# State stage of a Mamba layer: the copies of last columns two units later, the spread of C behind one more y addition, and four PSUM banks for the preparation of the first chunk

## The chip, the cores and the metric

The kernel runs on one core of a Trainium2 chip, as one program of five instruction streams: TensorE (PE), ScalarE (ACT), VectorE (DVE), GpSimd (POOL) and the DMA queues (SP). The metric is the device time of one execution in microseconds (us).

## The reference, cut to what matters

Six layers follow each other on x of shape (1, 1024, 256). The change touches the fifth, a Mamba layer:

```python
x = x + 0.5 * ffn(norm(x)); x = x + attention(norm(x)); x = x + 0.5 * ffn(norm(x))
x = x + 0.5 * moe(norm(x)); x = x + mamba(norm(x));     x = x + 0.5 * moe(norm(x))

# mamba, with DI = 512 inner channels, DN = 16 states, DR = 128
xz = h @ in_proj.T;  x, z = xz[..., :512], xz[..., 512:]
x_conv = silu(causal depthwise conv of x, 4 taps)
x_dbl = x_conv @ x_proj.T;  dt_low, Bm, Cm = split(x_dbl, [128, 16, 16])
delta = softplus(dt_low @ dt_proj.T + dt_bias);  A = -exp(A_log)
for l in range(1024):                       # the scan, for each channel d and state n
    hst[d, n] = exp(delta[l, d] * A[d, n]) * hst[d, n] + delta[l, d] * Bm[l, n] * x_conv[l, d]
    y[l, d] = sum_n hst[d, n] * Cm[l, n]
out = ((y + x_conv * D) * silu(z)) @ out_proj.T
```

All of it is in float32; matmuls that need the precision take a high and a low part of each operand and add three products.

## The kernel before

**Tiling.** The 1024 positions are two chunks of 512. Channels lie on the 128 partitions, in four tiles m = 0 to 3. PSUM has eight banks of 128x512 float32.

**Order of the work.** `steps()` yields one list of named steps for the whole program, and each engine runs through the same list and takes the steps that have a part for it, in that order. Waits on semaphores tie the engines together. So the order of this list sets the order on each engine, and an instruction that waits holds up everything behind it on its engine.

**Preparation.** `enter_steps` is the input projection, the convolution (w = 0 to 3, four VectorE instructions each, L1742 and L1744) and its silu (L1298). `dt_side(ch)` is a list of small steps: the high and low parts of x_conv (`xc2`); the product for dt (`xdt`) with its high copy on ScalarE (`dts`, L1302) and low part on VectorE (L1758); the same for B and C (`xbc`, `bct`, L1306 and L1764); the transposes of B and C (`trb`, read by `btx`, L1316); the four dt tiles (`dt`, three matmuls each) with two ScalarE readings each (`dta`, L1311 and L1312); the softplus in two sweeps of ScalarE (`dte`, `dtl`, L1325 and L1330), each with a load of another activation table; delta and delta times x_conv (`du`, L1773 and L1775, VectorE); and the transposes of the latter (`tru`, L424) with their copies (`dut`, L1320). All of these use one PSUM bank, number 7: `wait7` makes each use wait until the one before it in the plan has been read. For chunk 0 `alone` runs the steps of this list one after the other, each with its reader behind it, woven by `mamba_steps` between the input steps of chunk 1. For chunk 1 they run as side work between the units of chunk 0.

**State stage.** `state_steps(ch, side)` runs 64 units: pairs of states (n even, n odd), and within a pair the tiles m = 0 to 3 and in each the even and the odd state. Unit number k has u = k % 8. A unit consists of

- `ea`: exp(delta * A) on ScalarE (L1368); for an odd state it goes into PSUM bank 4 or 5, for an even one into SBUF
- b, which is delta * x_conv * B: for an even state four TensorE matmuls with a diagonal of B (`pb`, L1134, bank 4 or 5), for an odd one a GpSimd product (`bm`, L1916) with the row of B spread over the partitions
- `scan`: the recurrence on VectorE, L1797 for even and L1795 for odd states
- `cm`, one step later (GIVE = 1): the product with the spread row of C, for even states on GpSimd (L1925), for odd ones on VectorE (L1806), which reads C from PSUM bank 6
- `keep`, in the same step, chunk 0 alone: a ScalarE copy of the scan's last column (L1374), which chunk 1 starts from
- `ya`, three steps later (SUM = 3): TensorE adds the product to y in bank m (L1145); a float32 matmul shows as two records

The rows of B and C are spread by TensorE matmuls with a one-hot column: `spB` and `spC` through bank 7 and a ScalarE copy (L1115, L1337, L1344), and `bringC` for the odd states straight into bank 6 (L1122). The latter has to wait for the last product of the odd state before it (n - 2, m = 3), which still reads the bank. The scan of unit k waits for the product and the copy of unit k - 5, whose buffer it reuses, and an `ea` of an odd state or a `pb` waits for the scan two units back, whose bank it takes.

Of the kernel before, what the change touches and what calls it, by code (L numbers as in the profile page):

```python
# [6 lines left out]
F = mybir.dt.float32  # L7
# [279 lines left out]
def alone(side):  # L287
    for now, out in side:
        yield now + (out or [])
# [3 lines left out]
GIVE, SUM = 1, 3  # L293


def state_steps(ch, side):
# [6 lines left out]
    for k in range(n_units + SUM):  # L303
# [52 lines left out]
def build(nc, d):  # L356
# [11 lines left out]
    with ctx:  # L368
# [387 lines left out]
        def tensor_program():  # L756
# [28 lines left out]
            for x, *a in plan:  # L785
# [292 lines left out]
                elif x == "xdt":  # L1078
# [4 lines left out]
                    wait7(x, ch)  # L1083
                    pe.wait_ge(*xcd.at(ch, 3))
                    group(bank(7), [q for k in range(4) for q in three([w[:, k, 0:P] for w in X3], [v[:, k, :] for v in XC2])]).then_inc(*xdd.inc(ch))
                elif x == "xbc":
                    ch, = a
                    wait7(x, ch)
                    group(bank(7)[0:64, :], [q for k in range(4) for q in three([w[:, k, P:P + 64] for w in X3], [v[:, k, :] for v in XC2])]).then_inc(*xbd2.inc(ch))
                elif x == "dt":  # L1090
                    ch, m = a
                    wait7(x, ch, m)
                    if m == 0:
                        pe.wait_ge(*dtl.at(ch))
                    group(bank(7), three([w[:, m, :] for w in D3], DT)).then_inc(*dtm.inc(ch, m))
                elif x == "trb":
                    ch, = a
                    wait7(x, ch)
                    pe.wait_ge(*bcl.at(ch))
                    for i in range(TC):  # L1100
                        t = turn_over(bank(7)[:, i * P:i * P + P], BCs[ch][:, i * P:i * P + P].bitcast(F))
                    t.then_inc(*trb.inc(ch))
                elif x == "tru":
                    ch, i = a
                    wait7(x, ch, i)
                    if i == 0:
                        pe.wait_ge(*dud.at(ch, 3))
                    for m in range(4):
                        t = turn_over(bank(7)[:, m * P:m * P + P], uu[ch][:, m, i * P:i * P + P])
# [6 lines left out]
                elif x == "bringC":  # L1116
                    ch, n = a
                    if n > 1:
# [47 lines left out]
        ring7 = [x for x in plan if x[0] in after7]  # L1166

        def wait7(*here):
            k = ring7.index(here)
            if k:  # L1170
                name, *key = ring7[k - 1]
                out, done = after7[name]
                assert plan.index((out, *key)) < plan.index(here)
                pe.wait_ge(*done.at(*key))


        def scalar_program():
            for x, *a in plan:
# [120 lines left out]
                elif x == "dts":  # L1299
                    ch, = a  # L1300
                    act.wait_ge(*xdd.at(ch))
                    act.activation(DT[0], bank(7), ACT.Copy).then_inc(*dth.inc(ch))  # L1302
                elif x == "bct":
                    ch, = a
                    act.wait_ge(*xbd2.at(ch))
                    act.activation(BCs[ch][0:64, :], bank(7)[0:64, :], ACT.Copy).then_inc(*bch.inc(ch))  # L1306
                elif x == "dta":
# [3 lines left out]
                    act.activation(dl[ch][:, m, :], bank(7), ACT.Abs, bias=b)  # L1311
                    act.activation(uu[ch][:, m, :], bank(7), ACT.Relu, bias=b).then_inc(*dab.inc(ch, m))  # L1312
                elif x == "btx":
                    ch, = a
                    act.wait_ge(*trb.at(ch))
                    act.activation(BTh, bank(7).rearrange("p (t n) -> p t n", t=TC)[:, :, 0:64], ACT.Copy).then_inc(*btc.inc(ch))  # L1316
                elif x == "dut":
                    ch, i = a
                    act.wait_ge(*tru.at(ch, i))
                    act.activation(DUT[ch][i], bank(7), ACT.Copy).then_inc(*dut.inc(ch, i))  # L1320
# [60 lines left out]
        def vector_program():  # L1381
# [6 lines left out]
            for x, *a in plan:  # L1388
# [366 lines left out]
                elif x == "dts":  # L1755
                    ch, = a
                    dve.wait_ge(*dth.at(ch))
                    dve.tensor_tensor(DT[1], bank(7), DT[0].bitcast(F), ALU.subtract).then_inc(*dtl.inc(ch))  # L1758
                elif x == "bct":
# [4 lines left out]
                    dve.tensor_tensor(bc[32:64, :], bank(7)[32:64, :], bc[32:64, :].bitcast(F), ALU.subtract).then_inc(*bcl.inc(ch))  # L1764
# [247 lines left out]
```

## Time and profile before

| | us |
|---|---|
| median of 3 runs (lowest, highest) | 1063.16 (1059.86, 1063.55) |
| the profiled execution, its own time | 1064.1 |
| its span | 1062.8 |
| TensorE busy in the span (matmuls) | 763.3 (72%) |
| VectorE busy | 638.6 (60%) |
| ScalarE busy | 392.9 (37%) |
| GpSimd busy | 315.6 (30%) |
| mean granted TensorE clock | 0.843 of full speed |

All durations in the prediction come from the one profiled execution; its time includes 1.3 us around the span. The busy shares are means over stages with different limits, so they say little about one stage. The Mamba layer lies between about 560 and 928 us of the span. TensorE runs at one of two clock levels, 1.2 and 2.4 GHz; the granted clock is the mean share of the full speed in a stretch. In the rows a name such as FB<-PS is the tile written and the tile read, PS is PSUM, and "idle before" is in square brackets with the instruction that ended it. "Issue" means that the profile shows nothing that the engine waited for.

### The profile page before, as it was taken

Reading aid. Unit: us, or ns where it says so; the run is one execution under the profiler, and the core shown is the slowest. Engines: PE = TensorE matmul, PEld = TensorE weight load, DVE = VectorE, ACT = ScalarE, POOL = GpSimd, SP = SyncE. Lnnn points to the kernel's source line nnn. Section 1 sums busy time; section 2 is a strip of 40 time slices with the busy share of each in tenths; the row PEclk is TensorE's granted clock in tenths of the full one; section 3 lists DMA queues with packets and bytes.
Section 4 is the critical chain, followed back from the end, with each engine's and each line's share of the span. In section 5 each row is a group of like instructions: output and inputs, shape, how many; then the busy total and the mean of one; then the engine's idle time right before and its main releaser. Section 6 shows DMA issues by size and latency. Waiting matters only on the chain. (4 is left out here: it accounts for less than half of the span.)

```text
span 1062.8 us, 11266 instructions
## 1 busy us (share of the span) xinstructions
PE 763.3 (72%) x3818; PEld 547.8 (52%) x3818; DVE 638.6 (60%) x1069; ACT 392.9 (37%) x784; POOL 315.6 (30%) x373
## 2 busy tenths in 40 slices
PE   2866877589889597869329368678857888776980
PEld 2655654555554386758227135345535444465870
DVE  4976456665663385634256455588876878763332
ACT  3313353205556232223114544756443454120330
POOL 1241124100112210500320024357634567214005
PEclk9987599857999798889759568879979999968995
DMA  4600000000000230146310000000050000013334
GB/s 166 193 1 0 1 1 1 1 1 1 1 1 1 101 137 31 60 159 198 104 31 0 0 1 1 1 1 1 1 236 3 0 1 1 0 41 126 122 130 118
DMA packets 27816, 52.36 MB, mean 49 GB/s; under 512 B 2288, under 2 KB 22128, under 8 KB 26608
## 3 DMA queue, kind: packets, MB, share of 16 engines
q1 hardware_dynamic: 24688, 43.25, 11.6%
q0 software_dynamic: 3072, 8.39, 2.6%
q8 instruction: 32, 0.52, 0.2%
q14 instruction: 24, 0.20, 0.1%
HBM read 34.20 MB, written 17.43 MB: 49 GB/s over the span
## 5 line engine op out<-in xcount | busy, mean ns | idle before, releaser
L1145 PE MATMUL PS<-FB,C 128*128 128x512 f32 x256 | 135.4, 639 | 1.2 <-DVE FB L1806 1.2
L1241 ACT ACTIVATE FA<-PS 128x512 f32<-128x512 f32 (+3 forms) x192 | 82.7, 497 | 63.0 <-PE PS L922 61.9
L1888 POOL TENSOR_SCALAR_AFFINE_SELECT FA<-FA 128x128 f32<-128x128 f32 x128 | 36.9, 298 | 192.3 <-ACT FA L1241 190.7
L1925 POOL TENSOR_TENSOR FB<-FB,RBF 128x512 f32<-128x512 f32 x51 | 65.8, 1289 | 87.6 <-DVE FB L1797 87.6
L424 PE MATMUL PS<-C,FB 128*128 128x128 f32 x250 | 45.7, 307 | 56.2 <-DVE FB L1438 38.1
L897 PE MATMUL PS<-RA 128*128 128x128 f32 (+3 forms) x288 | 79.9, 402 | 4.1 <-DVE FA L1529 1.3
L922 PE MATMUL PS<-RA 128*128 128x512 f32 (+3 forms) x192 | 66.6, 408 | 17.0 <-ACT FA L1241 8.0
L897 PEld LDWEIGHTS PS<-RA 128*128 128x128 f32 x288 | 56.1, 242 | 31.3 <-DVE FA L1533 13.4
L424 PEld LDWEIGHTS PS<-C,FB 128*128 128x128 f32 x250 | 36.3, 160 | 68.1 <-DVE FB L1438 39.3
L1906 POOL DMA_INDIRECT FB<-GY,FB x32 | 30.6, 955 | 135.6 <-DMA GY<-FB 126.6
L1916 POOL TENSOR_TENSOR FB<-WE,FB 128x512 f32<-128x512 f32 x32 | 43.0, 1344 | 69.0 <-ACT FB L1337 69.0
L1045 PE MATMUL PS<-WE,FB 128*128 x248 | 62.7, 398 | 0.0
L1145 PEld LDWEIGHTS PS<-FB,C 128*128 128x128 f32 x256 | 46.7, 201 | 29.1 <-issue 16.3
L1684 DVE TENSOR_TENSOR FB<-FB,PS 128x256 f32<-128x256 f32 (+1 forms) x32 | 13.2, 412 | 72.7 <-ACT FB L1273 72.7
L922 PEld LDWEIGHTS PS<-RA 128*128 128x128 f32 x192 | 35.1, 201 | 39.6 <-ACT FA L1241 23.5
L420 PE MATMUL PS<-XN,RB 128*128 128x512 f32 x192 | 52.4, 435 | 2.1 <-DVE RB L1386 2.1
L1134 PEld LDWEIGHTS PS<-RBF,WE 128*128 128x128 f32 x256 | 36.8, 212 | 30.9 <-issue 14.0
L1045 PEld LDWEIGHTS PS<-WE,FB 128*128 128x128 f32 x248 | 46.9, 200 | 6.5 <-issue 0.8
L1134 PE MATMUL PS<-RBF,WE 128*128 128x128 f32 x256 | 38.7, 300 | 14.7 <-DVE FB L1797 11.1
L1533 DVE TENSOR_REDUCE FA<-PS 128x1 f32<-128x640 f32 (+2 forms) x48 | 44.3, 953 | 8.1 <-PE PS L897 7.8
L424 PE MATMUL PS<-C,RA 128*128 128x128 f32 x192 | 32.2, 326 | 21.9 <-ACT RA L1220 11.4
L1189 ACT ACTIVATE XN<-PS 128x512 fp32r<-128x512 f32 x24 | 13.6, 594 | 89.5 <-PE PS L424 89.4
(269 smaller groups left out, 1772.0 us busy)
## 6 DMA issues: line engine op xcount, KB each, us to landing
FB<-GX SPq DMA_DIRECT2D x14, 512.0 KB, 4.8
GY<-FB SPq DMA_DIRECT2D x14, 512.0 KB, 3.2
WE<-in_wr SPq DMA_DIRECT2D x4, 1536.0 KB, 11.3
WE<-in_wr SPq DMA_DIRECT2D x3, 2048.0 KB, 13.0
GX<-FA SPq DMA_DIRECT2D x1, 3968.0 KB, 14.0
FA<-in_w SPq DMA_DIRECT2D x2, 1024.0 KB, 7.6
FB<-in_we SPq DMA_DIRECT2D x4, 384.0 KB, 3.5
X<-in_x SPq DMA_DIRECT2D x2, 512.0 KB, 8.5
```

Source lines behind the costliest of these rows:

```text
L420: last = pe.matmul(out, a, b, start=start and i == 0, stop=stop and i == len(pairs) - 1, skip_group_check=skip)
L424: return pe.matmul(out, in_, ident, start=True, stop=True, is_transpose=True)
L897: return pe.matmul(out, QT[:, 4 * (g % 2) + hh, ii * P:ii * P + P], KT[:, 2 * g + hh // 2, c0:c1], start=start, stop=stop)
L922: pe.matmul(bk[:, c0:CH], KT[:, 2 * g + hh // 2, kt * P:kt * P + P], QT[:, 4 * (g % 2) + hh, c0:CH], start=True, stop=True).then_inc(*scs. ...
L1045: m = pe.matmul(bk[:, o:o + D], xt[:, o + k * P:o + k * P + P], WE[:, bass.ds(v + k * 256, 256)], start=k == 0, stop=k == 1)
L1134: t = pe.matmul(bank(4 + k % 2)[:, i * P:i * P + P], DUT[ch][i][:, m * P:m * P + P], dg[:, i * P:i * P + P], start=True, stop=True)
L1145: pe.matmul(bank(m), ident, shc[k % 4], start=n == 0, stop=n == DN - 1).then_inc(*yad.inc(ch, n, m))
L1241: act.activation(PT[n % 16][:, c0:], bank(4 + ring_no[(x, *a)] % 3)[:, c0:], ACT.Exp, scale=0.25).then_inc(*exd.inc(*a))
L1533: r = dve.reduce_max(N3[:, i, h:h + 1], bk.rearrange("p b n -> p (b n)")[:, 0:w], AX)
L1888: pool.affine_select(out=dd, in_=dd, compare_op=ALU.is_ge, fill=0.0, base=0, pattern=[[1, P]], channel_multiplier=-1).then_inc(*sel.inc(*a))
L1916: pool.tensor_tensor(sbb[k % 2], uu[ch][:, m, :], bs[(stb.no[ch, n] - 1) % 2], ALU.mult).then_inc(*bmd.inc(ch, n, m))
L1925: pool.tensor_tensor(shc[k % 4], sh[k % 5], Cs[(stc.no[ch, n] - 1) % 2], ALU.mult).then_inc(*cma.inc(ch, n, m))
```

## The change

1. `keep` moves from the step after its unit to the third step after it (KEEP = 3).
2. `bringC` was emitted at the step that holds the product of the last odd unit of the pair, which is the first step of the next pair (u = 0). Now it is emitted at the second step of the next pair (u = 1), ahead of that step's `ya`.
3. The preparation of chunk 0 gets an order of its own, `dt_alone`, and its eleven uses of bank 7 go round banks 4, 5, 6 and 7: each waits for the reader of the fourth use before it. The first use of bank 7 after them (the spread of B) waits for the readers of the last four, and the first `bringC` for the reader of the last transposes. Chunk 1's preparation still uses bank 7 alone.

```diff
--- before.py
+++ after.py
@@ -284,13 +284,21 @@
     return side
 
 
-def alone(side):
-    for now, out in side:
-        yield now + (out or [])
+def dt_alone():
+
+    for m in range(4):
+        yield [("xc2", 0, m)]
+    for x in (("xdt", 0), ("xbc", 0), ("dts", 0), ("bct", 0), ("dt", 0, 0), ("dt", 0, 1), ("dta", 0, 0), ("trb", 0), ("dt", 0, 2), ("dta", 0, 1),
+              ("btx", 0), ("dt", 0, 3), ("dta", 0, 2), ("dta", 0, 3), ("dte", 0), ("dtl", 0)):
+        yield [x]
+    for m in range(4):
+        yield [("du", 0, m)]
+    yield [("tru", 0, i) for i in range(TC)]
+    yield [("dut", 0, i) for i in range(TC)]
 
 
 UNITS = [(2 * p + j, m) for p in range(DN // 2) for m in range(4) for j in range(2)]
-GIVE, SUM = 1, 3
+GIVE, SUM, KEEP = 1, 3, 3
 
 
 def state_steps(ch, side):
@@ -314,10 +322,10 @@
         if 0 <= k - GIVE < n_units:
             n, m = UNITS[k - GIVE]
             out.append(("cm", ch, n, m))
-            if ch + 1 < NCH:
-                out.append(("keep", ch, n, m))
-            if n % 2 and m == 3 and n + 2 < DN:
-                out.append(("bringC", ch, n + 2))
+        if ch + 1 < NCH and 0 <= k - KEEP < n_units:
+            out.append(("keep", ch, *UNITS[k - KEEP]))
+        if k > 8 and u == 1 and k < n_units:
+            out.append(("bringC", ch, UNITS[k][0]))
         if 0 <= k - SUM < n_units:
             out.append(("ya", ch, *UNITS[k - SUM]))
         if held:
@@ -336,7 +344,7 @@
 
 def mamba_steps():
     yield [("An",)]
-    yield from weave((chain(enter_steps(0), alone(dt_side(0))), 1), (chain(([] for _ in range(8)), enter_steps(1)), 1))
+    yield from weave((chain(enter_steps(0), dt_alone()), 1), (chain(([] for _ in range(8)), enter_steps(1)), 1))
     yield from state_steps(0, dt_side(1))
     yield [("gate", 0)]
     yield from state_steps(1, leave_side())
@@ -1080,33 +1088,33 @@
                     if ch == 0:
                         pe.wait_ge(*mws.at(4))
                         pe.wait_ge(*xno.at(4, 1, 1))
-                    wait7(x, ch)
+                    bk = claim7(x, ch)
                     pe.wait_ge(*xcd.at(ch, 3))
-                    group(bank(7), [q for k in range(4) for q in three([w[:, k, 0:P] for w in X3], [v[:, k, :] for v in XC2])]).then_inc(*xdd.inc(ch))
+                    group(bk, [q for k in range(4) for q in three([w[:, k, 0:P] for w in X3], [v[:, k, :] for v in XC2])]).then_inc(*xdd.inc(ch))
...
                 elif x in ("spB", "spC"):
                     ch, n = a
@@ -1115,6 +1123,8 @@
                     pe.matmul(bank(7), HOT[:, h:h + 1].broadcast_to([P, P]), BCs[ch], start=True, stop=True).then_inc(*(spb if x == "spB" else spc).inc(ch, n))
                 elif x == "bringC":
                     ch, n = a
+                    if ch == 0 and n == 1:
+                        pe.wait_ge(*dut.at(0, TC - 1))
                     if n > 1:
                         pe.wait_ge(*cmb_.at(ch, n - 2, 3))
                     elif ch:
@@ -1163,15 +1173,30 @@
 
         after7 = {"spB": ("stB", stb), "spC": ("stC", stc), "mo": ("mox", mox), "tr1": ("xn", xno), "xdt": ("dts", dtl), "xbc": ("bct", bcl),
                   "dt": ("dta", dab), "trb": ("btx", btc), "tru": ("dut", dut)}
-        ring7 = [x for x in plan if x[0] in after7]
+        early7 = [x for x in plan if x[0] in after7 and x[1] == 0 and x[0] in ("xdt", "xbc", "dt", "trb", "tru")]
+        ring7 = [x for x in plan if x[0] in after7 and x not in early7 and x[0] not in ("xn",)]
+
+        def bank7(*here):
+            return bank(4 + early7.index(here) % 4) if here in early7 else bank(7)
+
+        def emptied(use, here):
+            name, *key = use
+            out, done = after7[name]
+            assert plan.index((out, *key)) < plan.index(here)
+            pe.wait_ge(*done.at(*key))
 
         def wait7(*here):
             k = ring7.index(here)
-            if k:
-                name, *key = ring7[k - 1]
-                out, done = after7[name]
-                assert plan.index((out, *key)) < plan.index(here)
-                pe.wait_ge(*done.at(*key))
+            for use in ring7[k - 1:k] if k else early7[-4:]:
+                emptied(use, here)
+
+        def claim7(*here):
+
+            if here not in early7:
+                wait7(*here)
+            elif early7.index(here) > 3:
+                emptied(early7[early7.index(here) - 4], here)
+            return bank7(*here)
 
 
         def scalar_program():
@@ -1299,25 +1324,25 @@
                 elif x == "dts":
                     ch, = a
                     act.wait_ge(*xdd.at(ch))
-                    act.activation(DT[0], bank(7), ACT.Copy).then_inc(*dth.inc(ch))
+                    act.activation(DT[0], bank7("xdt", ch), ACT.Copy).then_inc(*dth.inc(ch))
...
```

TensorE, turn from one pair of states to the next (L1134 is the b product of an even unit, L1115 the spread of B, L1122 the spread of C, L1145 a y addition), before:

```order
L1134 MATMUL PS<-RBF,WE 128x128 x4
L1115 MATMUL PS<-RB,HOT 128x512
L1122 MATMUL PS<-RB,HOT 128x512
L1145 MATMUL PS<-FB,C 128x512 x2
L1134 MATMUL PS<-RBF,WE 128x128 x4
L1145 MATMUL PS<-FB,C 128x512 x2
L1134 MATMUL PS<-RBF,WE 128x128 x4
```

and now, where the same instructions have the lines L1144, L1123, L1132 and L1155:

```order
L1144 MATMUL PS<-RBF,WE 128x128 x4
L1123 MATMUL PS<-RB,HOT 128x512
L1155 MATMUL PS<-FB,C 128x512
L1132 MATMUL PS<-RB,HOT 128x512
L1155 MATMUL PS<-FB,C 128x512
L1144 MATMUL PS<-RBF,WE 128x128 x4
L1155 MATMUL PS<-FB,C 128x512 x2
L1144 MATMUL PS<-RBF,WE 128x128 x4
```

One y addition has moved from behind the spread of C to ahead of it.

VectorE, preparation of chunk 0 (TENSOR_SCALAR and SCALAR_TENSOR_TENSOR are the convolution of chunk 1, the first TENSOR_TENSOR into RB the low part for dt, the 64x512 and 32x512 ones the low part of B and C, the one into RBF the sum of the transposed B, the one into WE the first of delta), before:

```order
L1742 TENSOR_SCALAR FB<-FB,C 128x512 x4
L1758 TENSOR_TENSOR RB<-PS,RB 128x512
L1744 SCALAR_TENSOR_TENSOR FB<-FB,C 128x512 x4
L1762 MEMSET RB 64x512
L1764 TENSOR_TENSOR RB<-PS,RB 32x512
L1744 SCALAR_TENSOR_TENSOR FB<-FB,C 128x512 x4
L1768 TENSOR_TENSOR RBF<-RBF 128x64
L1744 SCALAR_TENSOR_TENSOR FB<-FB,C 128x512 x4
```

and now:

```order
L1767 TENSOR_SCALAR FB<-FB,C 128x512 x4
L1769 SCALAR_TENSOR_TENSOR FB<-FB,C 128x512 x8
L1783 TENSOR_TENSOR RB<-PS,RB 128x512
L1769 SCALAR_TENSOR_TENSOR FB<-FB,C 128x512 x4
L1787 MEMSET RB 64x512
L1789 TENSOR_TENSOR RB<-PS,RB 32x512
L1793 TENSOR_TENSOR RBF<-RBF 128x64
```

The low part for dt stands behind eight convolution instructions (two of the sweeps) that followed it before, and that of B and C behind the whole convolution. On ScalarE the four silus of chunk 1 now stand ahead of the first reading of a dt tile, where they stood behind it, and the reading of the transposed B behind two dt tiles.

## Rows read from the trace of the kernel before

**Rows 1.** Busy time by stretch: us, PE, PEld, DVE, ACT, POOL, PEclk, DMA share, GB/s
```profile
578.00:624.00 46.00, 21.90 (x70) 13.09 (x68) 17.27 (x30) 23.07 (x39) 1.30 (x1) 0.62 0.00 0
624.00:770.00 146.00, 111.91 (x450) 68.73 (x451) 109.77 (x117) 79.91 (x194) 81.60 (x63) 0.89 0.00 1
785.00:916.00 131.00, 107.35 (x452) 64.50 (x451) 103.36 (x115) 57.67 (x106) 81.20 (x65) 0.93 0.10 41
```

**Rows 2.** Waits, state stage of chunk 0: waiter, releaser, us in total, times, longest
```profile
ACT SM L1374 <- DVE FB L1795: 21.2, 17, 3.9
...
PE PS L1122 <- DVE FB L1806: 16.5, 7, 5.2
```

**Rows 3.** Waits, state stage of chunk 1
```profile
PE PS L1122 <- DVE FB L1806: 14.0, 7, 2.3
```

**Rows 4.** Preparation in time: start, us, engine, line, what, count, [idle before <- releaser]
```profile
578.13 1.67 DVE L1742 TENSOR_SCALAR FB<-FB,C 128x512 f32<-128x512 f32 x4
...
582.05 0.69 DVE L1758 TENSOR_TENSOR RB<-PS,RB 128x512 fp32r<-128x512 f32 x1 [2.25 <-ACT RB L1302]
582.66 2.73 DVE L1744 SCALAR_TENSOR_TENSOR FB<-FB,C 128x512 f32<-128x512 f32 x4
...
591.05 2.29 ACT L1298 ACTIVATE FB<-FB 128x512 f32<-128x512 f32 x4
...
594.55 1.65 PE L420 MATMUL PS<-RB 128*128 128x512 f32 x3 [1.69 <-ACT WE L1312]
...
600.52 1.28 ACT L1325 ACT_TABLE_LOAD   x1
...
611.53 1.09 PE L424 MATMUL PS<-C,WE 128*128 128x128 f32 x4 [12.33 <-DVE WE L1775]
...
616.90 1.11 PE L424 MATMUL PS<-C,WE 128*128 128x128 f32 x4 [0.69 <-ACT WE L1320]
```

**Rows 5.** Transposes back to back elsewhere, TensorE in time
```profile
935.78 1.97 PE L424 MATMUL PS<-C,FB 128*128 128x128 f32 x8 [0.79 <-DVE FB L1438]
```

**Rows 6.** One turn of chunk 0 (k=40 to k=42), all engines in time
```profile
728.58 1.20 DVE L1797 TENSOR_TENSOR_SCAN FB<-RBF,PS 128x512 f32<-128x512 f32 x1
...
729.69 0.66 DVE L1806 TENSOR_TENSOR FB<-RBF,PS 128x512 f32<-128x512 f32 x1
...
729.99 0.71 ACT L1368 ACTIVATE FB<-WE,SM 128x512 f32<-128x512 f32 x1
...
730.41 0.50 PE L1122 MATMUL PS<-RB,HOT 128*128 128x512 f32 x1 [1.94 <-DVE FB L1806]
...
730.75 1.88 PE L1145 MATMUL PS<-FB,C 128*128 128x512 f32 x4
731.11 1.29 POOL L1916 TENSOR_TENSOR FB<-WE,FB 128x512 f32<-128x512 f32 x1
...
732.46 1.05 PE L1134 MATMUL PS<-RBF,WE 128*128 128x128 f32 x8
...
733.61 1.22 DVE L1797 TENSOR_TENSOR_SCAN FB<-FB,PS 128x512 f32<-128x512 f32 x1 [2.12 <-issue]
```

**Rows 7.** The additions behind the spread at five other turns, TensorE in time
```profile
669.78 2.89 PE L1145 MATMUL PS<-FB,C 128*128 128x512 f32 x4
...
799.62 3.02 PE L1145 MATMUL PS<-FB,C 128*128 128x512 f32 x4
...
824.05 3.56 PE L1145 MATMUL PS<-FB,C 128*128 128x512 f32 x4
...
858.15 3.52 PE L1145 MATMUL PS<-FB,C 128*128 128x512 f32 x4
...
901.69 2.69 PE L1145 MATMUL PS<-FB,C 128*128 128x512 f32 x4
```

**Rows 8.** The spread ahead of the fourth of these
```profile
857.82 0.50 PE L1122 MATMUL PS<-XN,HOT 128*128 128x512 f32 x1 [2.07 <-DVE FB L1806]
```

**Rows 9.** A turn of chunk 1 with a shorter wait
```profile
842.84 0.50 PE L1122 MATMUL PS<-XN,HOT 128*128 128x512 f32 x1 [1.27 <-DVE FB L1806]
```

More of the change, by code:

```diff
@@ L1082, in tensor_program @@
                         pe.wait_ge(*xno.at(4, 1, 1))
-                    wait7(x, ch)
+                    bk = claim7(x, ch)
                     pe.wait_ge(*xcd.at(ch, 3))
-                    group(bank(7), [q for k in range(4) for q in three([w[:, k, 0:P] for w in X3], [v[:, k, :] for v in XC2])]).then_inc(*xdd.inc(ch))
+                    group(bk, [q for k in range(4) for q in three([w[:, k, 0:P] for w in X3], [v[:, k, :] for v in XC2])]).then_inc(*xdd.inc(ch))
                 elif x == "xbc":
                     ch, = a
-                    wait7(x, ch)
-                    group(bank(7)[0:64, :], [q for k in range(4) for q in three([w[:, k, P:P + 64] for w in X3], [v[:, k, :] for v in XC2])]).then_inc(*xbd2.inc(ch))
+                    bk = claim7(x, ch)
+                    group(bk[0:64, :], [q for k in range(4) for q in three([w[:, k, P:P + 64] for w in X3], [v[:, k, :] for v in XC2])]).then_inc(*xbd2.inc(ch))
                 elif x == "dt":
                     ch, m = a
-                    wait7(x, ch, m)
+                    bk = claim7(x, ch, m)
                     if m == 0:
                         pe.wait_ge(*dtl.at(ch))
-                    group(bank(7), three([w[:, m, :] for w in D3], DT)).then_inc(*dtm.inc(ch, m))
+                    group(bk, three([w[:, m, :] for w in D3], DT)).then_inc(*dtm.inc(ch, m))
                 elif x == "trb":
                     ch, = a
-                    wait7(x, ch)
+                    bk = claim7(x, ch)
                     pe.wait_ge(*bcl.at(ch))
                     for i in range(TC):
-                        t = turn_over(bank(7)[:, i * P:i * P + P], BCs[ch][:, i * P:i * P + P].bitcast(F))
+                        t = turn_over(bk[:, i * P:i * P + P], BCs[ch][:, i * P:i * P + P].bitcast(F))
                     t.then_inc(*trb.inc(ch))
@@ L1108, in tensor_program @@
                     for m in range(4):
-                        t = turn_over(bank(7)[:, m * P:m * P + P], uu[ch][:, m, i * P:i * P + P])
+                        t = turn_over(bk[:, m * P:m * P + P], uu[ch][:, m, i * P:i * P + P])
                     t.then_inc(*tru.inc(ch, i))
@@ L1305, in scalar_program @@
                     act.wait_ge(*xbd2.at(ch))
-                    act.activation(BCs[ch][0:64, :], bank(7)[0:64, :], ACT.Copy).then_inc(*bch.inc(ch))
+                    act.activation(BCs[ch][0:64, :], bank7("xbc", ch)[0:64, :], ACT.Copy).then_inc(*bch.inc(ch))
                 elif x == "dta":
@@ L1315, in scalar_program @@
                     act.wait_ge(*trb.at(ch))
-                    act.activation(BTh, bank(7).rearrange("p (t n) -> p t n", t=TC)[:, :, 0:64], ACT.Copy).then_inc(*btc.inc(ch))
+                    act.activation(BTh, bank7("trb", ch).rearrange("p (t n) -> p t n", t=TC)[:, :, 0:64], ACT.Copy).then_inc(*btc.inc(ch))
                 elif x == "dut":
@@ L1319, in scalar_program @@
                     act.wait_ge(*tru.at(ch, i))
-                    act.activation(DUT[ch][i], bank(7), ACT.Copy).then_inc(*dut.inc(ch, i))
+                    act.activation(DUT[ch][i], bank7("tru", ch, i), ACT.Copy).then_inc(*dut.inc(ch, i))
                 elif x == "dte":
@@ L1757, in vector_program @@
                     dve.wait_ge(*dth.at(ch))
-                    dve.tensor_tensor(DT[1], bank(7), DT[0].bitcast(F), ALU.subtract).then_inc(*dtl.inc(ch))
+                    dve.tensor_tensor(DT[1], bank7("xdt", ch), DT[0].bitcast(F), ALU.subtract).then_inc(*dtl.inc(ch))
                 elif x == "bct":
@@ L1763, in vector_program @@
                     dve.wait_ge(*bch.at(ch))
-                    dve.tensor_tensor(bc[32:64, :], bank(7)[32:64, :], bc[32:64, :].bitcast(F), ALU.subtract).then_inc(*bcl.inc(ch))
+                    dve.tensor_tensor(bc[32:64, :], bank7("xbc", ch)[32:64, :], bc[32:64, :].bitcast(F), ALU.subtract).then_inc(*bcl.inc(ch))
                 elif x == "btx":
```

6 lines of the change are left out of this document (3 added, 3 removed).

## The prediction

> **What bounds the kernel now.** I read the views in this order: the busy time by stretch, the list of waits of the two state stretches, and then the instructions in order of time in the first chunk's preparation and around one turn from a pair of states to the next. The stretches that the change touches are the preparation of chunk 0 (46 us from 578 to 624), the state stage of chunk 0 (146 us) and that of chunk 1 (131 us) [rows 1]. In the preparation nobody is busy: TensorE 21.9 us, ScalarE 23.1, VectorE 17.3. It is a chain of hand-overs. In both state stretches VectorE (109.8 of 146, 103.4 of 131) and TensorE (111.9 and 107.4) are busiest, TensorE partly because it runs slowly, so what can be won there lies in VectorE's idle spells, 36 and 28 us.
>
> Where do they lie? TensorE waited seven times per chunk in L1122, the spread of C, for the product of VectorE: 16.5 us [rows 2] and 14.0 us [rows 3]. One such place in order of time is [rows 6]. With k the number of the unit, the scan of k=40 starts at 728.58, the product of k=39 runs behind it until 730.35, and only then may L1122 start (730.41, after 1.94 us of idle TensorE). Behind it in TensorE's queue stand two y additions (four records of L1145, 730.75 to 732.46, so 0.86 us for each addition) and the b product of k=42 (L1134, 1.05 us, done at 733.51). The scan of k=42 starts at 733.61, and VectorE had stood idle for 2.12 us before it. The other scans of this piece follow each other without a gap. So the wait that ends last there is TensorE's row of spread, two additions and b product, and its start is fixed by VectorE itself.
>
> **The change part by part.** *The spread of C.* The words of the change say that it goes behind the next pair's first b. The instruction order shows that it stood behind that b before as well; what it passes is one y addition (k=37 in the example) and nothing else. It happens at 14 turns, 7 in each chunk. The addition's input was ready long before, so it now fills part of the 1.94 us of waiting, and only one addition stands between the spread and the b product. Nothing is added, and no wait is new: the wait for the product of k=39 stays in front of the spread, and behind it are one addition, the side work of that unit and the b product. Who needs the spread is the VectorE product of k=41, which comes after the scan of k=42, so it isn't late. Worth: 0.86 us where TensorE runs at full clock, for VectorE's gap shrinks from 2.12 to 1.26 us. At five turns the four records took 2.89, 3.02, 3.56, 3.52 and 2.69 us instead of 1.88 [rows 7], because TensorE's clock fell to its lower level after the wait (the whole stretches were granted 0.89 and 0.93 [rows 1]); there half of the four is saved. A sixth turn, behind the longest wait of 5.2 us [rows 2], ran slowly too, but transposes behind it wait for VectorE's own work, so it counts at the full-clock price. Sum: 9 x 0.86 + (2.89 + 3.02 + 3.56 + 3.52 + 2.69)/2 = 7.7 + 7.8 = 15.5 us. The bound below is 14 x 0.86 = 12.0.
>
> What comes late next at such a turn? The exponential of k=42 is ready at 730.70 and GpSimd's product for k=43 at 732.40, over 2 us before the scan of k=43 would need it even then [rows 6]. Per eight units TensorE has to do 4 b products, 8 additions and 3 spreads, some 4 x 0.86 + 8 x 0.86 + 3 x 0.34 = 11.3 us (0.34 from the start of the spread at 730.41 to that of the addition, 730.75; a b product of 1.05 starts its successor a little before it ends). VectorE's period is eight scans of about 1.21 and four products of 0.66, each starting some 0.09 before the one ahead ends, with the gap of 2.12: 13.4 us now and 12.5 then. So TensorE still keeps up, at full clock.
>
> *The clock.* The idle spell of TensorE in front of the spread falls from about 2.0 us to about 1.1. The drop to the lower clock was seen after 2.07 us [rows 8], while the additions behind the waits of 1.27 us [rows 9] and 1.94 us [rows 6] aren't among the slow ones. If every drop went away, the remaining half of the five slow groups, 7.84 - 5 x 0.94 = 3.1 us, would go, and about as much again for the b products and side matmuls behind them: 6 us. If none goes, 0. I take the middle, 3 us, since 1.94 and 2.07 lie on either side and the new spell is nearer to 1.27. The Trainium skill, "TensorE: Matmul & The Clock Gate", Part 1, says that "the default state is throttled, and activity releases the throttle"; by it the denser queue would keep the full level and the whole 6 us would come. This case's rows don't decide it: spells that are nearly alike were followed by either level.
>
> *The copies of last columns (L1374), two units later.* ScalarE waited 21.2 us in 17 of them for scans [rows 2], but it has 66 us to spare in that stretch [rows 1]. What stands behind such a copy is the exponential for an odd unit, which waits for the same scan anyway (its PSUM bank), or side work whose input comes from TensorE. A copy is needed by the scan five units later, and its new place is still ahead of the exponential that this scan needs. I take 0; bounds from the 0.2 us of a copy and the few waits of VectorE for ScalarE: a gain of 1.5 us to a loss of 0.5.
>
> *Four banks for the preparation of chunk 0.* Two things move. First, the order on VectorE: before, the low part of dt's input (L1758, 582.05) ran between the convolutions of chunk 1, and VectorE idled 2.25 us ahead of it [rows 4]. Now eight convolution steps come first. VectorE is free at 578.13 + 1.67 = 579.8; eight steps at 2.73 for four, less the overlap, are 5.4, to 585.2; then 0.69 to 585.9 (3.2 us later than before); then four more steps to 588.6. The silu of chunk 1 (four in 2.29) follows the steps one by one and is done at about 589.3. Meanwhile TensorE has done the B and C rows without waiting, and from 585.9 the dt groups, 0.7 to 1.65 us each; two are done by 589.3 and none has to wait for a bank that isn't free. From there ScalarE is the bound: eight readings at 0.6 us (the four silus give its pace, 0.57) and the transposed B, 0.4, together 5.2, to 594.5. Before, the next step, the table load for the exponential, started at 600.52 [rows 4]. Gain 6.0.
>
> Second, the four groups of transposes from 611.53 on [rows 4]: one bank makes each wait for the copy before it, so they end at 616.90 + 1.11 = 618.01, 6.5 us after the first began. With four banks they run back to back, at half of 1.97 us each [rows 5], 3.9 us, and the copies follow behind. Gain 2.5. What follows (diagonals, spreads of B and C, the first scan) hangs on the last copy in the same way as before. Preparation together: 8.5 us. Bounds: 5.5, where half-clock dt groups hold up the last reading or a convolution waits, and 9.5.
>
> After the state stages everything is one chain up to the end (gate, projection, expert layer), so the gain isn't given back; the load of the expert weights starts with the gate of chunk 0 and moves with it.
>
> **Sum.** 8.5 + 15.5 + 3 + 0 = 27 us. The profiled execution took 1064.1 us with a span of 1062.8, with 1.3 around it, so it comes to 1037.1; it lay 0.9 above the median of the runs, 1063.16, so I predict 1036.
>
> **Rivals.**
> (a) The clock doesn't recover, or drops in other places, and the turns yield only their full-clock price: 8.5 + 12 = 20.5 us, 1042.7. For it: 1.94 and 2.07 us of idle gave both levels, so the length of that one spell isn't the whole cause.
> (b) The clock stays at its upper level throughout: 8.5 + 15.5 + 6 = 30 us, 1033. Against it: in the preparation TensorE idles for 12.3 us whatever the order [rows 4], and the state stage begins after it.
> (c) Another wait takes the place of the removed one at the turns (GpSimd's product or the exponential): then only the preparation counts, 1063.2 - 8.5 = 1054.7. Against it: the exponential was ready at 730.70 where the b product ended at 733.51 [rows 6].
> (d) Slower: TensorE stays at the lower level for whole pairs of states. Eight units then need about twice 11 us, 22, against 13.4 now: 8.6 us lost in each such period. With 16 periods in the two chunks, more than three further ones wholly at the lower level (27/8.6) would turn the gain into a loss; with five it is 1063.2 - 27 + 43 = 1079. Against it: the change makes TensorE's idle spells shorter, so nothing pushes it there.
>
> **How the numbers follow.** Forecast 0.55, (a) 0.25, (b) 0.12, (c) 0.05, (d) 0.03. With the bounds of the preparation and of the clock, from 5.5 + 12 = 17.5 to 9.5 + 15.5 + 6 + 1.5 = 32.5 us, the times are 1045.7 and 1030.7, and an us more for the executions' own spread gives the range 1030 to 1046. Case (c) and (d) stay outside. Within 0.5% is 1058 to 1068.5, about what a measurement of this kernel can tell from no change; only a mix of (c) and (d) ends there. Faster 0.95, same 0.03, slower 0.02.
>
> **What would show it.** In the changed profile, the seven scans per chunk that follow a turn should stand behind a gap near 1.26 us instead of 2.12, and one addition each should lie on either side of the spread. Table load at about 594.5, and the first scan 8.5 us earlier, if the preparation is right; VectorE's other scans spaced as before. The waits for the spread should add up to some 8 us per chunk instead of 16.5 and 14.0. The granted clock of the two state stretches shows which of forecast, (a) and (b) it is: near 0.95, 0.90 or 1.0. I am wrong if the turns keep their 2.12 us with another engine named behind them, or if the table load comes no earlier than 598.

## The result, and the profile after

| | before | after |
|---|---|---|
| median (lowest to highest), us | 1061.5 (1057.9 to 1063.6), 4 runs | 1032.0 (1027.2 to 1038.8), 4 runs |
| ratio, 95% interval | | 0.971 (0.966 to 0.977) |
| the profiled execution, its span | 1064.1, 1062.8 | 1032.8, 1031.6 |
| mean granted TensorE clock | 0.843 | 0.855 |

The median fell by 29.5 us; 1036 was forecast, in a range of 1030 to 1046. The ratio, here and below, is not the quotient of the two medians, so the two can differ by half a percent.

**Where it came from.** I cut the Mamba layer of both traces at the same four events: first convolution instruction of chunk 1, table load of the softplus, first scan, first gate product (and again the first scan and the gate for chunk 1). The lengths of the stages in us:

| | convolution to table load | to first scan | state stage 0 | between | state stage 1 |
|---|---|---|---|---|---|
| before | 22.4 | 23.3 | 146.0 | 15.2 | 130.7 |
| after | 16.0 | 20.1 | 136.6 | 15.2 | 119.3 |
| gain | 6.4 | 3.2 | 9.4 | 0.0 | 11.5 |

Together 30.5 of the 31.3 us that lie between the two profiled executions. VectorE and the clock in the stretches that answer to [rows 1] (columns as there), each cut at the events of the table:

```profile
578.00:614.63 36.63, 17.17 (x71) 12.09 (x69) 17.54 (x29) 22.81 (x39) 1.30 (x1) 0.74 0.00 0
614.63:751.24 136.61, 107.89 (x450) 65.28 (x450) 109.68 (x116) 77.99 (x194) 81.57 (x63) 0.93 0.00 1
766.41:885.66 119.25, 102.36 (x451) 62.14 (x450) 103.31 (x115) 57.66 (x106) 81.18 (x65) 0.96 0.11 45
```

VectorE idles 27 of 137 us and 16 of 119 where it had idled 36 of 146 and 28 of 131, with the same work done. The granted clock rose from 0.89 to 0.93 and from 0.93 to 0.96.

The waits for the spread of C, answering to [rows 2] and [rows 3], first chunk 0 and then chunk 1 (waiter, releaser, us in total, times, longest):

```profile
PE PS L1132 <- DVE FB L1831: 9.7, 7, 3.5
```
```profile
PE PS L1132 <- DVE FB L1831: 8.5, 7, 1.4
```

16.5 became 9.7 and 14.0 became 8.5, where "some 8 us" each was forecast. One turn of chunk 0 in order of time, answering to [rows 6] (TensorE, VectorE and the exponentials of ScalarE; L1132 is the spread, L1155 an addition, L1144 the b product, L1820 and L1822 the scans, L1831 VectorE's product):

```profile
712.25 1.02 PE L1155 MATMUL PS<-FB,C 128*128 128x512 f32 x2
712.54 1.19 DVE L1822 TENSOR_TENSOR_SCAN FB<-RBF,PS 128x512 f32<-128x512 f32 x1
...
713.65 0.66 DVE L1831 TENSOR_TENSOR FB<-RBF,PS 128x512 f32<-128x512 f32 x1
...
714.23 1.21 DVE L1820 TENSOR_TENSOR_SCAN FB<-PS,FB 128x512 f32<-128x512 f32 x1
...
714.37 0.50 PE L1132 MATMUL PS<-RB,HOT 128*128 128x512 f32 x1 [1.09 <-DVE FB L1831]
...
714.70 1.02 PE L1155 MATMUL PS<-FB,C 128*128 128x512 f32 x2
...
715.48 0.69 ACT L1393 ACTIVATE PS<-WE,SM 128x512 f32<-128x512 f32 x1 [0.82 <-DVE FB L1820]
715.56 1.05 PE L1144 MATMUL PS<-RBF,WE 128*128 128x128 f32 x8
...
716.70 1.22 DVE L1822 TENSOR_TENSOR_SCAN FB<-FB,PS 128x512 f32<-128x512 f32 x1 [1.26 <-ACT PS L1393]
```

One addition stands on either side of the spread, TensorE idles 1.09 us instead of 1.94, and VectorE's gap is 1.26 us instead of 2.12. The releaser that is named for it, the exponential, was done at 716.17; the b product ended at 716.61, and the scan started 0.09 later. The work that ends last there is still TensorE's row.

The preparation, answering to [rows 4]:

```profile
578.48 1.67 DVE L1767 TENSOR_SCALAR FB<-FB,C 128x512 f32<-128x512 f32 x4
...
580.19 5.52 DVE L1769 SCALAR_TENSOR_TENSOR FB<-FB,C 128x512 f32<-128x512 f32 x8
...
585.62 0.68 DVE L1783 TENSOR_TENSOR RB<-PS,RB 128x512 fp32r<-128x512 f32 x1
...
587.00 2.62 ACT L1323 ACTIVATE FB<-FB 128x512 f32<-128x512 f32 x4 [1.86 <-DVE FB L1769]
...
594.52 1.28 ACT L1350 ACT_TABLE_LOAD   x1
...
605.52 3.58 PE L432 MATMUL PS<-C,WE 128*128 128x128 f32 x16 [12.64 <-DVE WE L1800]
```

The idle of 2.25 us ahead of the low part is gone, the table load stands at 594.52, and the sixteen transposes run in one piece of 3.58 us where they had spread over 6.5.

One thing hadn't been forecast: the clock around the first scan. Windows of 6 us ahead of it, of the 8 us behind it, and of the next 8, first before and then after:

```profile
617.84:623.84 6.00, 4.32 (x13) 2.94 (x12) 0.00 (x1) 4.88 (x10) 1.30 (x1) 0.50 0.00 0
623.84:631.84 8.00, 5.19 (x19) 3.40 (x20) 7.93 (x9) 4.08 (x11) 4.47 (x4) 0.64 0.00 0
631.84:639.84 8.00, 4.45 (x15) 2.80 (x14) 7.42 (x9) 3.42 (x9) 3.86 (x3) 0.78 0.00 0
```
```profile
608.63:614.63 6.00, 3.54 (x15) 2.34 (x13) 0.00 (x0) 5.19 (x11) 1.30 (x1) 0.78 0.01 3
614.63:622.63 8.00, 4.97 (x19) 3.40 (x20) 7.93 (x9) 4.36 (x11) 4.47 (x4) 0.72 0.00 0
622.63:630.63 8.00, 4.44 (x19) 2.70 (x18) 7.93 (x10) 2.81 (x7) 3.88 (x3) 1.00 0.00 0
```

Behind the dense transposes TensorE is granted 0.78 ahead of the first scan, not 0.50, and 1.00 instead of 0.78 from 8 us behind it. The ninth scan starts 19.9 us after the first instead of 22.8: 2.9 us that belong to the preparation's change although they are won in the state stage. The ten profiles of this document agree on it. In the five with the four banks TensorE's clock rises to the full level 4.8 to 5.7 us ahead of the first scan, and the ninth scan follows the first by 19.9 us in each; in the five without them it rises 1.5 to 5.7 us behind the first scan, and the ninth scan follows by 22.4 to 22.8 us. It doesn't stay up at once: after the change it is low again from 2.3 us ahead of the first scan to 4.5 behind it, and before the change it was low again from 12.5 to 19.4 us behind it.

### The profile page after: what moved, and what is told of

It is laid out like the page before. It is cut to its first block and busy times, and to the rows that moved or that the text cites. A ratio compares the mean times of both kernels' runs of the same rounds, so it can differ in the third digit from the quotient of the medians.

```text
span 1031.6 us, 11267 instructions
## 1 busy us (share of the span) xinstructions
PE 750.4 (73%) x3818; PEld 542.1 (53%) x3818; DVE 638.6 (62%) x1069; ACT 390.6 (38%) x784; POOL 315.8 (31%) x373
## 5 line engine op out<-in xcount | busy, mean ns | idle before, releaser
L1155 PE MATMUL PS<-FB,C 128*128 128x512 f32 x256 | 132.3, 616 | 1.2 <-DVE FB L1831 1.2
L1155 PEld LDWEIGHTS PS<-FB,C 128*128 128x128 f32 x256 | 45.2, 196 | 20.9 <-issue 10.8
L1144 PEld LDWEIGHTS PS<-RBF,WE 128*128 128x128 f32 x256 | 35.6, 206 | 31.1 <-issue 14.0
L1144 PE MATMUL PS<-RBF,WE 128*128 128x128 f32 x256 | 37.8, 295 | 15.3 <-DVE FB L1822 11.8
```

Source lines behind the costliest of these rows:

```text
L1144: t = pe.matmul(bank(4 + k % 2)[:, i * P:i * P + P], DUT[ch][i][:, m * P:m * P + P], dg[:, i * P:i * P + P], start=True, stop=True)
L1155: pe.matmul(bank(m), ident, shc[k % 4], start=n == 0, stop=n == DN - 1).then_inc(*yad.inc(ch, n, m))
```

## The experiments

The parts were first run singly. The "stages" given with each are cut at the events of the table above, in the same order. Each experiment was timed against the kernel before on the same chip. That kernel's median was 1064.0 us over 19 runs (1053.8 to 1070.9) beside the first four experiments, and 1064.3 over 17 (1058.0 to 1070.4) beside the others.

**The spread of C alone (e1)**, on the kernel before:

```diff
-            if n % 2 and m == 3 and n + 2 < DN:
-                out.append(("bringC", ch, n + 2))
+        if k > 8 and u == 1 and k < n_units:
+            out.append(("bringC", ch, UNITS[k][0]))
```

> The kernel before with the spread of C behind one more y addition, and nothing else. If the spread is worth what the changed kernel's turns show (one addition out of VectorE's gap at each of 14 turns, and TensorE's clock kept up behind the shorter wait): the two state stretches shorter by about 9 and 11 us, the time about 21 us shorter, gaps of 1.26 and 1.20 us at the turns. If the clock recovered only because of the new copies or the new preparation: 12 to 16 us, with some groups of additions still at half rate.

Measured: 1043.3 us (1039.0 to 1046.7), ratio 0.982 (0.975 to 0.990). Stages: 22.4, 23.3, 139.0, 15.2, 118.8. So the preparation is as before, chunk 0 gains 7.0 and chunk 1 gains 11.9: 18.9 us (the ratio's 1.76% of 1064 is 18.7). Gaps at the last four turns of each chunk are 1.26 and 1.20 us. The additions behind the spread are slow at none of the 13 turns other than the third of chunk 0, so the clock's recovery there needs neither the copies nor the preparation. The 21 us of the expectation weren't reached. One reason is the first turn of chunk 0: its gap shrank by 0.87 us, but the stretch from the last scan ahead of it to the same place one pair on took 21.18 us instead of 20.98. The clock fell within it, behind another wait, that of TensorE for the low part of B and C (four transposes; first before, then e1):

```profile
657.72 0.63 PE L424 MATMUL PS<-C,XN 128*128 128x128 f32 x4 [2.52 <-DVE XN L1764]
```
```profile
657.46 1.09 PE L424 MATMUL PS<-C,XN 128*128 128x128 f32 x4 [2.53 <-DVE XN L1764]
```

The work behind the same wait ran at half rate in e1, and VectorE's gap ahead of the scan of k=12 grew from 1.86 to 2.92 us.

**The preparation alone (e2)**: the changed kernel with the old places of the copies and of the spread.

```diff
-        if ch + 1 < NCH and 0 <= k - KEEP < n_units:
-            out.append(("keep", ch, *UNITS[k - KEEP]))
-        if k > 8 and u == 1 and k < n_units:
-            out.append(("bringC", ch, UNITS[k][0]))
+            if ch + 1 < NCH:
+                out.append(("keep", ch, n, m))
+            if n % 2 and m == 3 and n + 2 < DN:
+                out.append(("bringC", ch, n + 2))
```

> The kernel before with the new preparation of chunk 0 alone. If the parts add: table load at about 594.5 and first scan at about 614.6, the state stretches as before, 9 to 10 us shorter in all. If the preparation also shifts TensorE's clock in the state stage, the turns at which additions run at half rate change too, by up to 6 us either way.

Measured: 1043.2 us (1040.8 to 1051.5), ratio 0.986 (0.977 to 0.994). Stages: 16.0, 20.1, 143.8, 15.2, 126.5. The preparation gains its full 9.5 us by itself, and the ninth scan again stands 19.9 us behind the first. Chunk 1, whose order is that of before, came out 4.2 us shorter in this profile. Its waits for the spread are as long as before (2.07 and 2.19 us at the first two turns), yet none of its additions ran slowly. I count that with the clock and not with the order of the work, which is unchanged there: e5, whose preparation has the same four banks, took 132.1 us for chunk 1. That the preparation has no hand in it is not shown, since the other profiles with the old order of chunk 1 (before, e3, e5, e8) took 130.6 to 132.1 us.

**The copies alone (e3)**: KEEP = 3 on the kernel before.

> The kernel before with the copies of last columns two units later, and nothing else. By the theory that nothing that VectorE waits for stands behind such a copy: no change, within 0.5 us in the state stretch of chunk 0. By the rival that ScalarE's waits on scans delay the side work of chunk 1: up to 3 us shorter, with VectorE's gaps behind ScalarE smaller.

Measured: 1062.6 us (1058.1 to 1067.2, 10 runs), ratio 0.999 (0.995 to 1.003). Stages: 22.4, 23.3, 145.7, 15.2, 130.8. ScalarE hardly waits in the copy any more, but waits for the same scans in the exponential that stands behind it, as the list of its waits in chunk 0 shows (L1368 is the exponential; compare the first row of [rows 2]):

```profile
ACT PS L1368 <- DVE FB L1795: 31.5, 18, 5.7
```

All its waits for scans in that stage are 39 us instead of 51, and its waits for products of TensorE 28 us instead of 14: it waits elsewhere, and no less.

**The changed kernel with the copies at their old place (e7)**: KEEP = 1.

> The changed kernel with the copies of last columns back at their old place. If the copies are worth nothing: the same as the changed kernel, the state stretch of chunk 0 within 0.5 us of 136.6. If they matter only once the turns are short: 1 to 3 us longer.

Measured: 1032.1 us (1031.6 to 1036.3), ratio to before 0.970 (0.965 to 0.975), that of the changed kernel being 0.971; state stages 136.6 and 119.2. The stages of the changed kernel are 136.6 and 119.3, so the copies are worth nothing in either company.

**Banks with the old order (e5)**: the changed preparation with `alone(dt_side(0))` in place of `dt_alone()`, spread and copies as before.

```diff
-    yield from weave((chain(enter_steps(0), dt_alone()), 1), ...
+    yield from weave((chain(enter_steps(0), alone(dt_side(0))), 1), ...
```

> The kernel before with the eleven uses of chunk 0's preparation going round four banks, but in the old order (each reader right behind its use, the low part for dt between the convolutions), and nothing else. If the banks free the transposes and lift TensorE's clock, and the order frees the dt tiles: the last four copies end about 2.5 to 3 us earlier relative to the table load, the dt tiles gain some 3 us of the 6 (TensorE runs ahead, ScalarE's readings follow each other), the first scan comes 5.5 to 7 us earlier, and the first nine scans take 2 to 3 us less. If the order alone does it: 2.5 us from the transposes and nothing before the table load.

Measured: 1060.6 us (1050.8 to 1062.9, 10 runs), ratio 0.993 (0.989 to 0.997). Stages: 18.3, 20.2, 146.0, 15.2, 132.1. So of the 6.4 us ahead of the table load 4.1 come from the banks and 2.3 from the new order on top of them (the new order with one bank was not run), and the 3.2 us behind it are the banks'. The ratio's 0.7% is 7.1 us, the preparation's 7.2. The state stages gain nothing in this profile although the first units are 2.9 us quicker here too: three more turns than before ran at the low clock (counted in the next section).

**Filling the wait (e4)**: the kernel before, where the spread of B, which stands ahead of the wait, is issued five times over into the same bank from the second pair on. The wait in front of the spread of C gets shorter, but nothing starts earlier.

```diff
+                    for _ in range(4 if x == "spB" and n > 1 else 0):
+                        pe.matmul(bank(7), HOT[...], BCs[ch], start=True, stop=True)
                     pe.matmul(bank(7), HOT[...], BCs[ch], start=True, stop=True).then_inc(...)
```

> The kernel before, with the matmul that spreads B issued five times over instead of once from the second pair of states on (the same result written to the same bank), which fills about 0.9 us of the wait ahead of the spread of C and moves nothing else. If it is the idle spell that lets the clock fall: the additions behind the spread run at full rate at all turns (1.88 us for four records), VectorE's gaps there are 2.1 us throughout, and the time is 5 to 9 us shorter though TensorE does more. If the clock falls for another cause: the same five slow turns, or others, and 0 to 2 us longer.

Measured: 1058.1 us (1049.3 to 1062.9, 10 runs), ratio 0.995 (0.991 to 0.999), so some 5 us shorter with 56 matmuls more. The state stages took 144.6 and 126.0 us, 1.4 and 4.7 less. The last turn of each chunk has no spread of B left to fill it, and at the third of chunk 0, filled too, the wait is still 3.49 us and the additions are slow. Here are, in chunk 0, a filled turn and the unfilled one (TensorE; the line numbers are shifted, L1124 is the spread of C and L1147 an addition):

```profile
746.88 0.50 PE L1124 MATMUL PS<-RB,HOT 128*128 128x512 f32 x1 [1.01 <-DVE FB L1808]
...
760.40 0.50 PE L1124 MATMUL PS<-RB,HOT 128*128 128x512 f32 x1 [2.18 <-DVE FB L1808]
...
760.74 3.23 PE L1147 MATMUL PS<-FB,C 128*128 128x512 f32 x4
```

The gaps of VectorE at the fourth to sixth turn, all filled, are still 2.12 us; behind the unfilled seventh the additions are slow and the gap is 3.80.

**The kernel before once more (e8)**, for one profile.

> The kernel before, profiled again. If the turns at which TensorE falls to its lower clock hang on chance (where its changes of level fall), other turns are slow than the five of the first profile, or fewer; the stage lengths differ by as much as the slow groups say, some 1.6 us each. If they hang on the order of the instructions alone, the same five are slow.

Measured: 1070.2 us, span 1069.0. Stages: 22.4, 23.3, 148.9, 15.2, 130.6. The preparation comes out the same to 0.1 us. Neither case of the expectation fits by itself: the five slow turns of the first profile are slow again, and two more turns of chunk 0 with them, at waits of the same length. One of the two is the very turn of [rows 6], and the wait there is again 1.94 us:

```profile
733.97 0.50 PE L1122 MATMUL PS<-RB,HOT 128*128 128x512 f32 x1 [1.94 <-DVE FB L1806]
```

Its row of four addition records took 2.60 us, 0.65 a record, where that of [rows 6] took 1.88, 0.47 a record. The preparation itself began at 582.0 instead of 578.1; over all ten profiles it began between 571.4 and 584.2, though the code ahead of it is the same. Two profiled spans therefore differ by up to 13 us for a reason that no edit here touches, and I compare stage lengths.

**The spread really behind the next b product (e6)**: the changed kernel with the spread one step later, so that TensorE has both additions and the b product of k=42 ahead of it.

```diff
-        if k > 8 and u == 1 and k < n_units:
-            out.append(("bringC", ch, UNITS[k][0]))
+        if k > 8 and u == 2 and k < n_units:
+            out.append(("bringC", ch, UNITS[k - 1][0]))
```

> The changed kernel with the spread of C one step later still, so that it stands behind the b product of the next pair's second even unit (k = 8p + 2), which then no longer waits for it. If the row of spread, addition and b product is what the remaining gap of 1.2 us consists of: no gap at most turns, 12 to 17 us less than the changed kernel, about 1017. If TensorE (11.3 us per eight units against VectorE's 11.2) is the bound that comes next: half of it, 6 to 8 us, with small gaps spread over all even units. If VectorE's product of k = 8p + 1 then waits for the late spread: no gain, the gap moves to that product.

Measured: 1018.0 us (1013.8 to 1020.6, 6 runs), ratio to before 0.957 (0.953 to 0.960). It is the fastest of all, 14 us below the changed kernel, whose interval of 0.966 to 0.977 it doesn't touch. Stages: 16.0, 20.1, 128.4, 15.2, 109.4. The last four turns of each chunk have no gap left. One of them (TensorE, VectorE and one exponential in time):

```profile
709.33 1.05 PE L1144 MATMUL PS<-RBF,WE 128*128 128x128 f32 x8
...
709.56 1.21 DVE L1820 TENSOR_TENSOR_SCAN FB<-PS,FB 128x512 f32<-128x512 f32 x1
...
710.13 0.48 PE L1132 MATMUL PS<-RB,HOT 128*128 128x512 f32 x1
...
710.45 1.88 PE L1155 MATMUL PS<-FB,C 128*128 128x512 f32 x4
...
710.69 1.19 DVE L1822 TENSOR_TENSOR_SCAN FB<-FB,PS 128x512 f32<-128x512 f32 x1
710.81 0.69 ACT L1393 ACTIVATE PS<-WE,SM 128x512 f32<-128x512 f32 x1 [0.82 <-DVE FB L1820]
```

The b product is done at 710.38, ahead of the scan that needs it, and the spread has no idle time in front of it. The scan at 710.69 starts before the exponential at 710.81, of the same line as the one that the profile had named as releaser in the changed kernel: it wasn't the cause. By the order of the kernel it couldn't be: it is that of the odd unit k=43, and the scan of k=42 doesn't read it. The stretch that answers to the last of [rows 1] was granted the full clock:

```profile
758.00:867.00 109.00, 98.35 (x450) 59.66 (x450) 102.35 (x115) 57.72 (x106) 81.06 (x65) 1.00 0.11 47
```

VectorE is now busy 102 of 109 us there: it is the bound of this stage.

## Why the prediction was right

**The spread: right, with its size.** The step said that one addition passes at 14 turns and the gap shrinks from 2.12 to 1.26 us. It does, and e1 has nothing else in it. Cut turn by turn, e1 gained 11.8 us at the five turns that had been slow and 7.0 at the other nine, with 0.2 in the first pair. For the nine the prediction had 9 x 0.86 = 7.7; the difference is the first turn of chunk 0, which came out 0.2 us longer instead of 0.86 shorter, less 0.3 us beyond the price at the third. For the five it had 7.8 and, with the clock's 3, 10.8.

**The clock: the middle value fits; what turned it is now known better.** At full clock the five would have gained 5 x 0.86 = 4.3 us, so 7.5 of the 11.8 are the clock's. The price of a slow turn can be read from e2, where the same turns weren't slow: VectorE's gap is 2.06 us instead of 3.75 at the fourth turn of chunk 1 and 2.82 instead of 4.46 at the second of chunk 0, 1.6 to 1.7 us a turn and about 8.3 for five. The prediction had 3.5 (7.8 less 4.3) + 6 = 9.5 for the case that every drop goes, so its 6 was too large and its 3 too small: 4.0 of what it called 6 was won. That the middle came so near is in part luck, because how many slow turns there are to win differs between profiles of one kernel (5, and 7 in e8). To see what it hangs on, I took from all ten profiles the first addition records behind each spread of C (at full clock 0.47 us each in a row of four, 0.51 in a row of two, 0.59 alone), and called a row slow where its records took 0.65 us or more on the mean. The third turn of chunk 0, with its long wait, is left out, and so is e6, which has no such wait:

| idle spell of TensorE in front of the spread | in | turns | slow behind it |
|---|---|---|---|
| 0.63 to 1.44 us | after, e1, e7; e4's filled turns; one turn each of before, e3, e5, e8 | 54 | 0 |
| 1.71 to 2.30 us | before, e2, e3, e5, e8; e4's unfilled turns | 63 | 27 |

With the spread moved only two records stand directly behind it, but the stretch behind them tells the same: the granted clock is 1.00 throughout the 5 us that follow the spread at each of the 54 turns. Among the longer spells the outcome isn't fixed: before had 5 such slow turns, e3 5, e8 7, e5 8 and e2 only 1. Nor are they drawn turn by turn: the five of before are slow in e3, e5 and e8 as well, and e2, with waits of the same length at these five, has none of them slow and another one instead. So rival (a), that the drops would stay or move, is out for the turns: behind a shorter spell none was seen. Elsewhere a new drop did come, in e1 and e2, behind the wait of 2.5 us in front of the transposes of B and C. Rival (b), the full clock throughout, is nearly right in chunk 1 (0.96) and not in chunk 0 (0.93), where the third turn still waits 3.50 us and the chunk still starts below full clock; over both stages the mean is the 0.95 that the prediction had named for its own case. e4 shows the effect by itself: with the waits filled and the order unchanged, 6.1 us went from the state stages in the profile, and 0.5% (0.1 to 0.9) from the time. The Trainium skill, "TensorE: Matmul & The Clock Gate", Part 1, has that activity releases the throttle. The useless matmuls of e4 agree with it: no drop behind 11 filled turns, four of which had slow additions in the profile of before. By it the whole 6 us were to come instead of the 3 that I took. At the five turns, where every drop went, 4.0 came: the direction is as the page has it, and the 6 was my own estimate.

**The preparation: right in place, too small in size.** The table load was forecast at 594.5 in a profile whose convolution starts at 578.13, 16.4 us behind it, and came 16.0 behind it; the transposes were forecast to take 3.9 us and took 3.58. The term was 8.5 us. It measured 9.5 up to the first scan (6.4 instead of 6.0, and 3.2 instead of 2.5), the upper bound given, and, with the first units' 2.9, 12.4. The missing step is that of the clock: the prediction let the change touch it only at the turns, and used "in the preparation TensorE idles for 12.3 us whatever the order" as a reason against more. That spell is still there (12.64 us), but behind it the clock now rises as the dense transposes end, 5.7 us ahead of the first scan. e2 and e5, both with the banks, have it (0.78 and 0.90 in the 6 us ahead of the first scan); e1 without them has 0.50. That the banks do it is shown; that it is the density of the transposes, and nothing else that the banks move, is argued from the order in time. The prediction also put its 6.0 us down to "the order on VectorE", though it reckoned with free banks. That was wrong in its cause: e5 gives two thirds of the gain ahead of the table load to the banks.

**The copies: right.** 0 was taken; e3 gives 0.999 (0.995 to 1.003), and e7 leaves the changed kernel where it is.

**The sum.** By the stages 30.5 us went where 27 were added up: 9.5 for 8.5 in the preparation, and 20.9 for 18.5 in the state stages. The latter are the 18.9 of e1, 2.4 more in chunk 0 and 0.4 less in chunk 1. So what lay beyond the forecast is for the most part the preparation, directly and through the clock behind it. The singles don't just add. e2 gained 2.2 + 4.2 us in the state stages beside the preparation; both it and e1 took away slow turns of chunk 1, which can go only once. Stage by stage chunk 1 gives 11.9 in e1, 4.2 in e2, and 11.5 with both. Of the 4.0 us between 1036 and 1032.0, 1.7 are only that the kernel before had a median of 1061.5 in the runs beside the changed one and not 1063.16. The range, by its own words, should have gone to 1046.7, and it left out the 0.5 us that the copies might cost; neither matters here.

**The rivals (c) and (d)** didn't occur. What none of the cases saw is that the remaining gap of 1.26 us was still to be had. The prediction noted that only one addition passes and stopped there; the same row, read on, says that the b product needn't stand behind the spread at all, which e6 turned into another 14 us.

**What stays open.** Why 27 of the 63 longer spells were followed by the lower clock and the others not: the same turn, with the same wait, went either way in two profiles of one kernel. Nor is it known what makes the same five turns slow in four profiles and none of them in a fifth. And at the first two turns of chunk 0 VectorE still waits 4.02 and 1.95 us after the change. There side work for chunk 1 stands between the addition and the b product, twelve matmuls at the first (2.8 us of the gap) and three at the second (0.7 us); to move it was not tried.

## What to carry to other kernels

When an instruction has to wait for another engine, look at what stands behind it in its queue and is ready: the price isn't the wait but everything that starts late behind it. Move it behind the ready work whose reader is waiting first; here passing one addition gave 0.86 us a turn, and passing the b product too took the whole gap at the last four turns of each chunk. On TensorE count a second gain if the wait gets short enough that the clock stays up, also in the stage that follows the denser work, and judge by stage lengths and several profiles, since the same turn with the same wait can go either way.

## What the runs showed of the hardware that had not been expected

- Behind idle spells of 0.63 to 1.44 us in front of the spread none of 54 turns ran at the lower clock, behind 1.71 to 2.30 us 27 of 63 did. Profiles with the same order of work at the turns had 1 to 8 of them, four of these profiles the same five.
- Sixteen transposes in one piece of 3.58 us, after 12.64 us of idle, were followed by a granted clock of 0.78 in the 6 us ahead of the first scan; with a wait between each four of them, after 12.33 us of idle, it was 0.50.
- Adding work can save time: 56 useless matmuls (four of them took 1.18 us at a turn of full clock) made the kernel 0.5% (0.1 to 0.9) faster.
- The named releaser of a gap can be wrong where two producers end close together: an exponential done 0.53 us before the scan started was named, and in e6 the scan of such a turn started ahead of the same exponential.
